# Expert weights spread over partitions by DMA from SBUF rows, in place of selector matmuls

## The reference

```
combine = zeros(T, E).at[arange(T)[:, None], topk_idx].add(topk_w)
up      = einsum('th,ehi->eti', x, expert_up)
down    = einsum('eti,eih->eth', silu(up), expert_down)
moe_out = einsum('te,eth->th', combine, down)
```

## Time and profile before

| | |
|---|---|
| median of 3 runs | 1341.64 us |
| the profiled execution | 1341.54 us |
| its span | 1339.8 us |
| mean granted TensorE clock | 0.944 |
| TensorE / VectorE / ScalarE / GpSimd busy | 87% / 57% / 51% / 27% |
| DMA moved | 16.27 MB, of it 14.74 MB by the queue of SP |

### The profile page before, as it was taken

How to read it: one execution, slowest core, us unless ns; L and a number is a source line. 1 busy time by engine, 2 the same in 40 slices (tenths; PEclk the granted TensorE clock), 3 DMA queues, 4 the chain that set the end, 5 groups by cost and what they waited for, 6 DMA issues and landing times. The chain is left out here.

```text
span 1339.8 us, 24482 instructions
## 1 busy us (share of the span) xinstructions
PE 1169.1 (87%) x9672; PEld 847.5 (63%) x9697; DVE 766.5 (57%) x1671; ACT 685.7 (51%) x1205; POOL 364.8 (27%) x340
## 2 busy tenths in 40 slices
PE   1878998489999999999998689978548997999998
PEld 0667367378888888888885546653224665466666
DVE  5867534455556556565562369983636997622223
ACT  1677630155665656656564246656205665644441
POOL 3200001122232222322222232201653320644441
PEclk9999898699999999999998889999858998999999
DMA  4500000100000000000000000000000000000000
GB/s 162 185 1 1 0 1 1 63 1 1 1 1 2 1 1 1 2 1 1 1 1 1 0 1 2 2 2 0 1 0 2 2 1 2 1 0 8 9 0 16
DMA packets 6526, 16.27 MB, mean 12 GB/s; under 512 B 1312, under 2 KB 3568, under 8 KB 5520
## 3 DMA queue, kind: packets, MB, share of 16 engines
q1 hardware_dynamic: 6416, 14.74, 3.0%
HBM read 13.69 MB, written 1.05 MB: 11 GB/s over the span
## 5 line engine op out<-in xcount | busy, mean ns | idle before, releaser
L1102 POOL TENSOR_TENSOR work<-work 128x1024 f32<-128x1024 f32 x64 | 121.4, 1897 | 324.8 <-DVE work L1181 324.8
L1168 DVE TENSOR_REDUCE work<-psum 128x8 f32<-128x1024 f32 x64 | 77.9, 1217 | 108.9 <-PE psum L1000 108.9
L1179 DVE TENSOR_REDUCE work<-work 128x8 f32<-128x1024 f32 x64 | 77.7, 1214 | 73.3 <-ACT work L1119 73.3
L1119 ACT ACTIVATE work<-work 128x1024 f32<-128x1024 f32 x64 | 67.3, 1052 | 98.4 <-DVE work L1172 98.4
L1495 PEld LDWEIGHTS psum<-w_down,work 128*128 128x128 f32 x768 | 101.8, 195 | 24.9 <-issue 21.7
L887 ACT ACTIVATE work<-psum 128x512 f32<-128x512 f32 x128 | 72.9, 596 | 66.4 <-PE psum L777 65.5
L1495 PE MATMUL psum<-w_down,work 128*128 128x128 f32 x768 | 102.8, 279 | 1.7 <-DVE x L1580 0.7
L1572 DVE TENSOR_TENSOR work<-psum,big 128x512 f32<-128x512 f32 x67 | 45.8, 689 | 89.1 <-PE psum L1475 55.9
L919 DVE TENSOR_REDUCE work<-psum 128x8 f32<-128x1024 f32 x64 | 75.4, 1220 | 32.9 <-PE psum L765 18.8
L777 PEld LDWEIGHTS psum<-ident,work 128*128 128x128 f32 x512 | 56.7, 142 | 43.3 <-issue 29.9
L1172 DVE TENSOR_TENSOR work<-psum,work 128x1024 f32<-128x1024 f32 x64 | 78.4, 1225 | 6.4
(11 more groups left out here) (319 smaller groups left out, 2554.9 us busy)
## 6 DMA issues: line engine op xcount, KB each, us to landing
x<-in_x SPq DMA_DIRECT2D x1, 1024.0 KB, 5.0
ctx_tok<-in_ctx SPq DMA_DIRECT2D x1, 1024.0 KB, 6.8
ctxt<-in_ctxt SPq DMA_DIRECT2D x1, 1024.0 KB, 10.4
mask<-in_mask SPq DMA_DIRECT2D x1, 1024.0 KB, 7.0
w_down<-in_down SPq DMA_DIRECT2D x1, 1024.0 KB, 6.2
ctx_tok<-in_g SPq DMA_DIRECT2D x1, 1024.0 KB, 4.9
big<-in_u SPq DMA_DIRECT2D x1, 1024.0 KB, 6.9
out<-x SPq DMA_DIRECT2D x4, 256.0 KB, 2.2
```

The source lines that it names most:

```text
L1102: pool.tensor_tensor(prob[:, u % 2, h, :], prob[:, u % 2, h, :], rinv[:, u % 2, h].unsqueeze(2).broadcast_to([P, 8, P]), ALU.mult)\
L1168: dve.tensor_reduce(nmax[:, u % 2, h], s, AX.X, ALU.max, negate=True).then_inc(S["max"], 1)
L1179: dve.tensor_reduce(rsum[:, u % 2, h], prob[:, u % 2, h, :], AX.X, ALU.add).then_inc(S["sum"], 1)
```

## The change

The router's weights stay float32. The split into three terms is gone, `turn_back` transposes the float32 values, and `combt` holds one float32 row per expert (32 rows). The select matmuls and the selectors are gone. In their place SP issues DMA transfers within SBUF: for every weighted tile the expert's row of 512 tokens (2 KB) is read once for each of its 64 or 128 partitions and written into one of four `spread` buffers. There are two transfers of 128 KB per tile in `f0` and `f3`, one of 256 KB in `f2`. A tile's transfer waits until the multiply four tiles before it has read its buffer, and for the first tile of a group until `combt` holds that group. The multiply takes the weights from `spread` in SBUF and no longer from PSUM. In `f3` the store of a group stands in the same queue, behind the ninth tile of the next group.

```
-        self.sels = sb("sels", [P, 2048], BF16)
-        self.combt = sb("combt", [P, T], BF16)
+        self.combt = sb("combt", [32, T])
...
     def turn_back(self, pe, g):
...
         for c in range(GB):
-            mm = pe.matmul(k.bank[7][0:rows, c * P:(c + 1) * P],
-                           self.parts[:, GB * g + c, :, :].rearrange("p q e -> p (q e)"), k.ident16[:, :],
-                           start=True, stop=True)
+            mm = pe.transpose(k.bank[7][0:self.E, c * P:(c + 1) * P], self.w[:, GB * g + c, :], k.ident[:, :])
...
-        link(dve.tensor_copy(parts[:, :, 0, :], w))
-        link(dve.tensor_tensor(low, w, parts[:, :, 0, :], ALU.subtract))
-        link(dve.tensor_copy(parts[:, :, 1, :], low))
-        dve.tensor_tensor(parts[:, :, 2, :], low, parts[:, :, 1, :], ALU.subtract).then_inc(S["parts"], 1)
...
+    WR = 4
+    spread = a.take(WR * GT, "p (n c) -> p n c", n=WR) if routed else None
+    landed = [k.sem(f"{tag}_weights{n}") for n in range(WR)]
...
-            def select(n):
-                g, j = divmod(n, J)
-                if weighted[j]:
-                    c = made(n) - 1
-                    pe.wait_ge(r.S["comb"], g + 1)
-                    if c >= 2:
-                        pe.wait_ge(S["made"], c - 1)
-                    pe.matmul(bank[4 + c % 2][:, :], tiles[j][3], k.combt[:, g * GT:(g + 1) * GT],
-                              start=True, stop=True).then_inc(S["sel"], 1)
...
             def weigh(n):
                 c = made(n) - 1
-                dve.wait_ge(S["sel"], c + 1)
+                dve.wait_ge(landed[c % WR], 16 * len(tiles[n % J][3]) * (c // WR + 1))
...
-                dve.tensor_tensor(h3[:, c % 3, :], bank[4 + c % 2][:, :], ring[n % R], ALU.mult)\
+                dve.tensor_tensor(h3[:, c % 3, :], spread[:, c % WR, :], ring[n % R], ALU.mult)\
                    .then_inc(S["made"], 1)
...
+            for n in weighted_tiles if routed else ():
+                g, j = divmod(n, J)
+                c = made(n) - 1
+                if j == 0:
+                    sp.wait_ge(r.S["comb"], g + 1)
+                if c >= WR:
+                    sp.wait_ge(S["made"], c - WR + 1)
+                width = P // len(tiles[j][3])
+                for half, e in enumerate(tiles[j][3]):
+                    sp.dma_start(spread[half * width:(half + 1) * width, c % WR, :],
+                                 k.combt[e:e + 1, g * GT:(g + 1) * GT].unsqueeze(1).broadcast_to([1, width, GT]))\
+                      .then_inc(landed[c % WR], 16)
+                if last_sub and g and j == 8:
+                    store(g - 1)
```

More of the change, by code:

```diff
@@ L717, in small_head_attention @@
          ("setup", "stepped", "zero", "proj", "k", "q", "v", "km", "vp", "score", "max", "sub", "exp", "turn", "pt", "pv",
-          "inv", "on", "out", "added", "stated", "xb", "sel")}
+          "inv", "on", "out", "added", "stated", "xb")}
     def fills(b):
@@ L1208, in _ @@
                     total(u, 1)
[L1213 to L1230, removed]
 class Route:
@@ L1245, in __init__ @@
         self.st = a.take(GT)
-        self.s, self.w, self.low = take(E), take(E), take(E)
+        self.s, self.w = take(E), take(E)
         self.base = take(E) if rbias is not None else self.s
@@ L1274, in turn_back @@
     def turn_back(self, pe, g):
-        k, S, rows = self.k, self.S, 3 * self.E
+        k, S = self.k, self.S
         pe.wait_ge(S["parts"], 1)
@@ L1294, in keep @@
     def keep(self, act, g):
-        k, S, rows = self.k, self.S, 3 * self.E
+        k, S = self.k, self.S
         act.wait_ge(S["turn2"], g + 1)
-        act.activation(k.combt[0:rows, g * GT:(g + 1) * GT], k.bank[7][0:rows, :], ACT.Copy)\
+        act.activation(k.combt[0:self.E, g * GT:(g + 1) * GT], k.bank[7][0:self.E, :], ACT.Copy)\
            .then_inc(S["comb"], 1)
@@ L1301, in choose @@
         k, S, E, G, best = self.k, self.S, self.E, self.G, self.best
-        s, v, w, low, tot, base, rep, parts = (self.s, self.v, self.w, self.low, self.tot, self.base, self.rep,
-                                               self.parts)
+        s, v, w, tot, base, rep = self.s, self.v, self.w, self.tot, self.base, self.rep
         done = [0]
@@ L1354, in choose @@
             mark(rep, v, E, self.top)
-            link(dve.scalar_tensor_tensor(out=w, in0=rep[:, :, 0:E], scalar=self.MARK, in1=v[:, :, 0:E],
-                                          op0=ALU.is_equal, op1=ALU.mult))
+            dve.scalar_tensor_tensor(out=w, in0=rep[:, :, 0:E], scalar=self.MARK, in1=v[:, :, 0:E],
+                                     op0=ALU.is_equal, op1=ALU.mult).then_inc(S["parts"], 1)
         else:
@@ L1389, in choose @@
             link(dve.tensor_scalar(tot, tot, self.factor, None, ALU.mult))
-            link(dve.tensor_tensor(w, w, wide(tot, E), ALU.mult))
-        link(dve.tensor_copy(parts[:, :, 0, :], w))
-        link(dve.tensor_tensor(low, w, parts[:, :, 0, :], ALU.subtract))
-        link(dve.tensor_copy(parts[:, :, 1, :], low))
-        dve.tensor_tensor(parts[:, :, 2, :], low, parts[:, :, 1, :], ALU.subtract).then_inc(S["parts"], 1)
+            dve.tensor_tensor(w, w, wide(tot, E), ALU.mult).then_inc(S["parts"], 1)
 def feed_forward(k, tag, sub, tiles, function, ahead, one_down=False, routing=None, spare=(), bias=None):
@@ L1667, in _, with store @@
                     reciprocal_root(g)
-        if last_sub:
-            @block.sync
-            def _(sp):
-                for g in range(NG):
-                    sp.wait_ge(S["added"], g + 1)
-                    sp.dma_start(k.out[:, g * GT:(g + 1) * GT], k.x[:, g * GT:(g + 1) * GT])\
-                      .then_inc(S["stored"], 16)
+        @block.sync
+        def _(sp):
+            def store(g):
+                sp.wait_ge(S["added"], g + 1)
+                sp.dma_start(k.out[:, g * GT:(g + 1) * GT], k.x[:, g * GT:(g + 1) * GT]).then_inc(S["stored"], 16)
+            for n in weighted_tiles if routed else ():
[12 more added lines that the diff above has]
+                    store(g - 1)
+            if last_sub:
+                store(NG - 1)
                 sp.wait_ge(S["stored"], 16 * NG)
@@ L1762, in build @@
             k.stage(normalise, "n1", k.x, k.xn, k.xnt)
-            tiles = [(cut("up0", j), None, None, k.sels[:, j * P:(j + 1) * P], cut("down0", j))
+            tiles = [(cut("up0", j), None, None, (2 * j, 2 * j + 1), cut("down0", j))
                      for j in range(8)]
@@ L1786, in build @@
             tiles = [(cut("ew2", j), k.cols[:, C_EB + j:C_EB + j + 1], None,
-                      k.sels[:, j * P:(j + 1) * P], w["comb2"][:, :]) for j in range(8)]
+                      (j,), w["comb2"][:, :]) for j in range(8)]
             k.stage(feed_forward, "f2", 5, tiles, ACT.Silu, ahead=16, one_down=True,
@@ L1793, in build @@
             k.stage(small_head_attention, "a3", 6, ("wq3", "wk3", "wv3", "wo3"), k.col("bq3"), k.col("bk3"),
-                    k.rows[:, R_BV3:R_BV3 + P], k.gated_bo[:, 1, :], k.key_mask_rows, k.set_key_mask, 3,
-                    (32, 64))
+                    k.rows[:, R_BV3:R_BV3 + P], k.gated_bo[:, 1, :], k.key_mask_rows, k.set_key_mask, 3)
         if stages > 7:
             k.stage(normalise, "n7", k.x, k.xn, k.xnt)
-            tiles = [(cut("g3", j), None, cut("u3", j), k.sels[:, j * P:(j + 1) * P], cut("down3", j))
+            tiles = [(cut("g3", j), None, cut("u3", j), (2 * j, 2 * j + 1), cut("down3", j))
                      for j in range(16)]
```

16 lines of the change are left out of this document (3 added, 13 removed).

## The result

The changed kernel takes 2119.44 us (median of 4 runs, 2114.33 to 2123.93), the kernel before beside it 1342.47 us (4 runs, 1341.59 to 1346.26). The ratio is 1.578, with a 95% interval of 1.573 to 1.583: 777 us more. The direction and the mechanism are those of the prediction, and the time lies in its range; the point forecast, 2318 us, was 199 us too high, and 2119 also lies under the 2250 to 2400 us of the case that I had taken as likeliest.

The account below looks back on a forecast made before the run. TensorE (87% busy) was taken as the bound before, DMA spreads after. Stage terms of +249.4, +259.3 and +469.4 us with small corrections made +977.0 on 1341.5, so 2318 us; range 1350 to 2800 us.

Parts of the forecast that it names:

- the case that I had taken as likeliest: Spreads in the expert stages: T from 9.3 to 10.5 us, 2250 to 2400 us in all, chance 0.60.
- T: Time that one 256 KB spread takes from its source row in the expert stages, taken as 9.83 us.
- (d): Expert stages: 128 added spreads of 256 KB; no stage can be shorter than its number of spreads times T.
- (iii): SBUF source row yields one of sixteen equal parts of full DMA flow, 26.7 GB/s: T is 9.83 us; the one taken.
- (ii): Mask spread from one DRAM row: 129 GB/s with engines busy 0.41 of the time, 2.0 us for 256 KB.
- (a): Expert stages: 128 selector matmuls removed, 26.9 us of TensorE, a gain only where TensorE still sets the pace.
- (b): Transposes back, 12 sets of four now in float32: 0.44 us a set against 0.22, +0.7 us in the sum.
- (c): Four VectorE operations of the split leave the end of the routing chain: priced at nothing, covered by the ups.
- the formula: Whole kernel: time is 1060 + 128 T, giving 2318 us.
- No limit, with the collision: Expert stages: no source row limit, but VectorE and GpSimd collide, +19.3 us in the second: 1344 us, chance 0.05.
- No limit and no collision: Expert stages: T near 0.7 to 1.5 us and hidden, TensorE sets the pace: 1325 us, chance 0.09.
- Rows in DRAM: SBUF row serves like a DRAM row, T about 2.0 us: 1356 us; chance 0.12 with everything up to 9.3 us.

Follow-up runs that it names:

- many source rows: Changed kernel with each spread read from 64 or 128 rows of a weight tile instead of one row of weights: 1345.65 us.
- the last experiment: Kernel before, with spreads only in the third expert stage, read from float32 rows kept in DRAM; bf16 selectors in the first two stages: 1335.75 us.
- one SBUF input: Kernel with many source rows, but the multiply reads a PSUM bank in place of the spread: 1331.88 us.
- rows placed apart: Changed kernel with expert rows placed so that successive tiles read from different groups of four neighbouring rows: 1622.66 us.

## Why the prediction was right, and where not

**The rate, T.** The step that was mis-sized is (d), the term 128 T, with T = 9.83 us. Measured it is 8.25, and 1060 + 128 x 8.25 = 2116 us. The choice between the bounds, (iii) rather than (ii), was right: with many source rows 774 us vanish, with DRAM rows 767. It was a choice, as no row of the trace before read a single SBUF row; what shows it is the experiments, not the argument made for it. But a sixteenth of the full flow, 26.7 GB/s, is the rate of one path, and the sum let every spread run at it. That holds only while neighbours follow each other (9.6 us, 27.3 GB/s). Wherever the source is about to change to another four rows, both paths work for a while, and a step takes some 6.3 us in place of 9.7 (2.6 to 7.5 us in the second stage). Why it is the last tile of the old rows that gains, and not the first of the new ones, no run tells. My guess, not shown, is that the 16 engines do not run level, and the late ones have the path to themselves when the early ones have moved on. I had both facts in hand, sixteen paths and a ring that lets SP run ahead, and did not ask what the next tile reads.

"SBUF — State Buffer", section "Door 1: The DMA port swizzle", of the Trainium skill gives the port of rows 0 to 3 a rate of 27.2 GB/s; within four rows the trace agrees (27.3 GB/s). Its grouping also fits the places of the short steps. The 2294 us that I worked out by it was too high for the same reason as my own sum: it used the port's rate and left out that successive tiles change ports.

**The stages**, by first issue to last multiply: forecast 316, 316 and 631 us from the first copy, measured 262, 276 and 519. In proportion to the spreads, as a rate demands. The second is the slowest per spread because there only one tile in four is the last of its rows, against one in two.

**The landing.** I expected about 39 us, four spreads deep. Measured: 15.1 us for 128 KB and 28.5 for 256 KB. A full ring holds eight transfers in the first and third stage, and it was not what filled up. SP was held in the issue itself: a median of 4.8 us and up to 9.7 us, against the 0.44 of the earlier trace rows that I had counted. Landing over issue time gives some 3 transfers in flight. My 0.44 us for an issue, and 0.88 us per tile, was wrong tenfold, and cost nothing, as little but the next spread stands behind it.

**The evidence of idle engines.** I had argued (ii) from a share of 0.41 at 129 GB/s. In the stages after, the share is 0.88 at 33 GB/s. A slow source does not show as idle DMA engines here. And the DRAM rows of the last experiment give a share of 0.37 at 117 GB/s, the same rate for a share as 0.41 at 129, in a stage that TensorE paces. So the low share need be no sign of a limit at the row, and that argument gave the right direction by luck.

**(a), (b), (c) and the leftovers.** The freed 26.9 us of TensorE gave nothing where DMA paces, as forecast; the attention stages kept their length (448.77 and 449.33 us). The 8.25 us also hold each stage's first landing, which the formula counts once more; without it 1060 + 1051.5 = 2112 us, against the 2114.33 of the execution from which these steps are read. That this closes within 3 us is partly cancellation. The start of the first stage came 2.6 us later than before (forecast 0.2). From last multiply to the next first issue it took 0.9 us more and 3.6 us less (forecast 0.7 and 1.9 less). From the last multiply to the end of the span it took 1.2 us more (forecast 0.9 less), mostly because the last matmuls ran at the lower clock: the last eight took 1.91 us against 1.06 in the earlier trace rows. I had said that TensorE would fall to about half of the span; it fell to 61%, since the span is shorter than forecast and its matmuls between waits run at the lower clock. I had also named a lower granted clock as something that would prove the sum wrong; it came inside the expert stages (0.52 to 0.68), where it is covered but for those last matmuls, and in the attention stage measured above the clock is 1.00 before and after.

**The rivals** were measured by the experiments. No limit, with the collision: forecast 1344, measured 1345.65 with many source rows. No limit and no collision: forecast 1325, measured 1331.88 with one SBUF input. Rows in DRAM: 1356, measured 1352.8. The collision's price per addition was forecast as a whole multiply, 0.69 us; the turns of 1.94 us are just that, but not all 28 additions pay it (the shortest took 1.26 us): forecast 19.3 us, measured 12.6 in the stage. So 1344 came out as near as it did partly because the gain without a collision was also smaller than forecast. "SBUF — State Buffer", section "Who interferes with whom", of the Trainium skill has VectorE with two SBUF inputs and GpSimd share a read port that is held for a whole instruction; the trace agrees (1.25 + 0.69 against 1.41 us).

## What to carry to other kernels

Before a transfer takes over work from an engine, ask how many different places of SBUF it reads at a time, not how many bytes it moves: a broadcast out of one row ran at 27 GB/s, out of eight alternating places at 65, and out of 64 or more rows, or one row in DRAM, it no longer set the pace (117 GB/s in the last experiment's third stage). In this kernel a spread paid with its rows in DRAM, and only in the stage where the engine that it relieves is the bound. And price the cases that you don't believe in: the three rivals came within 7 us of their runs and turned out to be a map of the alternatives.

## What the runs showed that I had not expected

- Transfers that follow each other overlap when their source rows lie in different groups of four, at 44 to 76 GB/s against 27: steps of 6.3 instead of 9.7 us, and 4.1 when every tile changes its place. Out of the same four rows they gain nothing. Cut into 64 KB pieces they are 8 to 9% faster where two experts' rows take turns, and take half as long again where four pieces in a row read one row.
- An issue on SP is not a fixed 0.44 us: with slow transfers ahead of it, it lasted 4.8 us in the median and 9.7 us at most.
- The DMA share is not a flow: 0.88 at 33 GB/s, 0.88 at 67 (rows placed apart), 0.37 at 117 with spreads from DRAM (the third stage of the last experiment, 1178 to 1327 us).
- Sixteen places of source rows are no better than eight (1634.63 and 1622.66 us).
